# Five first gathers instead of two ahead of the last scatters, between the two runs of expert tiles

## The reference, cut to what matters

```python
x = x + _L0_conv_ref(_ln_c(x), ...)              # gate per channel
t = _to_tokens(x)                                # [2, 4096, 128]
t = t + _L0_ffn_ref(_ln_t(t), ...)               # experts, layer 0
x = _from_tokens(t, x)
x = x + _L1_conv_ref(_ln_c(x), ...)              # max-pools of 7 sizes, weighted per channel
t = _to_tokens(x)
t = t + _L1_ffn_ref(_ln_t(t), ...)               # experts, layer 1
# an expert: h = gelu(t @ W1[e] + b1[e]);  y = h @ W2[e] + b2[e], weighted, two of eight per token
```

## Time and profile before

| what | value |
|---|---|
| median of three executions | 989.05 us (987.12 to 992.66) |
| span of the profiled execution | 1121.3 us |
| TensorE matmul busy | 810.7 us, 72% of the span |
| GpSimd busy | 616.5 us, 55% |
| VectorE busy | 565.6 us, 50% |
| ScalarE busy | 516.3 us, 46% |
| mean granted TensorE clock | 0.844 of full speed |

### The profile page before, as it was taken

The page is one execution under the profiler, slowest core; times in us unless marked ns, Lnnn a source line. Parts: engine busy times, 40 slices in busy tenths (PEclk is TensorE's granted clock), DMA queues, the critical chain, the costliest instruction groups (busy, mean ns, idle before and its releaser), DMA issues.

```text
span 1121.3 us, 14549 instructions
## 1 busy us (share of the span) xinstructions
PE 810.7 (72%) x4233; PEld 683.7 (61%) x4233; DVE 565.6 (50%) x1308; ACT 516.3 (46%) x1407; POOL 616.5 (55%) x590
## 2 busy tenths in 40 slices
PE   1854389897867867986689488975996677796780
PEld 0434268785767655864678376854786565674670
DVE  8957902280500291999775296999681003300005
ACT  1405045562444445653266156643393443453563
POOL 1000266676655675788623755888646466665640
PEclk9876579997988888998589689998798788998895
DMA  8001344453565742553137733543256446555456
GB/s 317 1 0 57 123 149 125 139 156 98 174 193 187 248 156 87 172 158 118 38 109 236 254 110 109 183 138 102 65 162 220 135 128 201 194 157 174 133 162 225
DMA packets 54557, 165.23 MB, mean 147 GB/s; under 512 B 13632, under 2 KB 13645, under 8 KB 54224
## 3 DMA queue, kind: packets, MB, share of 16 engines
q1 hardware_dynamic: 36304, 128.87, 34.6%
q0 software_dynamic: 18176, 35.44, 10.8%
HBM read 134.89 MB, written 31.20 MB: 148 GB/s over the span
## 4 chain that ended last, share of the span: by engine, by line
PE 40%; DVE 26%; ACT 10%; another core or an unknown queue 10%; issue 8%; DMA 3%; POOL 2%; SPq 0%; POOLq 0%; ACTq 0%; DVEq 0%
PE h_ps L783 14%; PE yT_ps L796 12%; DVE state L1302 6%; DVE work L1288 4%; DVE work L1283 4%; ACT hT L596 4%; PE turn_ps L718 4%; PE acc_ps L735 3%; DVE tok L1252 2%; PE acc_ps L755 2%; DVE work L1296 2%; PE xT_ps L772 2%; ACT yT L607 1%; PE h_ps L886 1%
## 5 line engine op out<-in xcount | busy, mean ns | idle before, releaser
L511 POOL DMA_INDIRECT xg<-xn_rows,tile_rows x284 | 305.4, 1075 | 243.1 <-DVEq L1218 126.6
L520 POOL DMA_INDIRECT y_rows<-yr,tile_rows x284 | 306.9, 1080 | 236.1 <-ACT yr L616 147.5
L783 PE MATMUL h_ps<-xT,expert 128*128 128x256 f32 (+1 forms) x1376 | 317.7, 381 | 64.9 <-ACT hT L596 37.7
L796 PE MATMUL yT_ps<-hT,expert 128*128 128x256 f32 (+1 forms) x1376 | 300.2, 369 | 34.9 <-ACT yT L607 21.6
L596 ACT ACTIVATE hT<-h_ps,expert 128x256 f32<-128x256 f32 (+1 forms) x688 | 250.7, 451 | 154.7 <-PE h_ps L783 70.0
L783 PEld LDWEIGHTS h_ps<-xT,expert 128*128 128x128 f32 x1376 | 244.4, 213 | 103.1 <-issue 52.6
L796 PEld LDWEIGHTS yT_ps<-hT,expert 128*128 128x128 f32 x1376 | 247.5, 209 | 71.6 <-ACT yT L607 26.1
L1252 DVE SCALAR_TENSOR_TENSOR tok<-work,share,tok 128x128 f32<-128x128 f32 x224 | 61.2, 346 | 340.3 <-DMA work<-y_rows 336.9
L607 ACT ACTIVATE yT<-yT_ps,expert 128x256 f32<-128x256 f32 (+1 forms) x172 | 72.9, 444 | 170.3 <-PE yT_ps L796 92.4
L584 ACT ACTIVATE xT<-xT_ps 128x256 f32<-128x256 f32 x144 | 56.4, 392 | 117.8 <-PE xT_ps L772 59.7
L772 PE MATMUL xT_ps<-ident,xg 128*128 128x128 f32 x284 | 61.2, 298 | 58.2 <-DMA xg<-xn_rows,tile_rows 45.4
(11 more groups left out here) (210 smaller groups left out, 661.1 us busy)
## 6 DMA issues: line engine op xcount, KB each, us to landing
expert<-in_experts SPq DMA_DIRECT2D x172, 514.5 KB
work<-y_rows SPq DMA_DIRECT2D x24, 512.0 KB
xn_rows<-work SPq DMA_DIRECT2D x16, 512.0 KB, 4.4
xg<-xn_rows,tile_rows POOLq DMA_INDIRECT x284
y_rows<-yr,tile_rows POOLq DMA_INDIRECT x284
tok<-in_x_tokens SPq DMA_DIRECT2D x8, 512.0 KB, 6.9
state<-in_x SPq DMA_DIRECT2D x2, 2048.0 KB, 17.1
work<-y_rows SPq DMA_DIRECT2D x16, 256.0 KB, 6.1
```

Of the source, the lines that this page charges most:

```text
L511: pool.indirect_dma_start(xg[:, s, h, :], None, xn_rows[unit], bass.IndirectOffsetOnAxis(ap=tile_rows[unit % 2][:, at, 0, h:h + 1], axis=0)) \
L520: pool.indirect_dma_start(y_rows[unit], bass.IndirectOffsetOnAxis(ap=tile_rows[unit % 2][:, at, 1, h:h + 1], axis=0), yr[:, s, h, :], None ...
L783: mm = pe.matmul(h_ps[c // 2][:, c % 2, cols], expert[:, t.load(h) % W_RING, c * P:(c + 1) * P], xT[:, t.slot(2), cols], start=True, stop= ...
L796: mm = pe.matmul(yT_ps[:, cols], expert[:, t.load(h, d) % W_RING, HIDDEN + c * P:HIDDEN + (c + 1) * P], hT[:, s, c, cols], start=(c == 0), ...
```

## The change

`G_FIRST` goes. `begin` of a run's first unit gathers all five tiles at once, and nothing is left to gather at the top of the unit's loop. For unit 0 the order of the DMAs is what it was, as no scatter stands between. For unit 2 the gathers of tiles 2, 3 and 4 come ahead of the scatters of unit 1's tiles 33, 34 and 35. The number of DMAs and every other engine's program are the same.

```diff
-G_FIRST = 2
...
             for u in range(UNITS):
                 if begins_run(u):
                     if u == 0:
-                        begin(u, range(G_FIRST))
-                    for d in range(G_FIRST, G_AHEAD):
-                        gather(Tile(u, 0), d)
+                        begin(u, range(G_AHEAD))
...
                     if t.s == t.last + 1 and u + 1 < UNITS:
-                        begin(u + 1, range(G_FIRST))
+                        begin(u + 1, range(G_AHEAD))
                     if t.has(-S_BEHIND) and t.at(-S_BEHIND)[1] < TILES - 1:
                         scatter(t, -S_BEHIND)
                     if t.has(-2) and t.at(-2)[1] == TILES - 1:
                         scatter(t, -2)
```

## The result

The changed kernel takes 997.97 us (median of 18 executions, 993.95 to 1004.57), the kernel before, run beside it, 989.45 us (18 executions, 986.93 to 999.69). The ratio is 1.0082 with a 95% interval of 1.0057 to 1.0106: 8 us slower (5.6 to 10.5), where 7.3 were forecast. All 284 gathers and 284 scatters are still there; only their order at one place is new.

A forecast was written before the change was run, and what follows sets the result against it. No single engine bounds it: TensorE's and VectorE's paths meet at `gap`, VectorE's later. Its scatters' +7.57 us counts fully, TensorE's -5.24 us nothing; taken as 7.3, 989.05 + 7.3 = 996.4 us, range 986.5 to 999.5.

The forecast's parts named there:

- The clash in the queue: GpSimd's queue at the break before unit 2: gathers forward, TensorE -5.24 us; five scatters back, VectorE +7.57 us.
- Who sets `gap`: At unit 2's channel means: VectorE's path is already later by 3.5 us, so its full +7.57 us counts.
- VectorE's path: From unit 1's scatters through output loads, combine and normalising to the channel means: 674.3 before, 681.9 after, without stalls.
- The sum without stalls: Both paths to the channel means with profile stalls removed: TensorE 670.8, VectorE 674.3 before; 665.6 and 681.9 after.
- TensorE's path: From tile 2's gather through turning the normalised tokens at step 7 to the channel means: 670.8 before, 665.6 after.
- the lead of 3.5: At the channel means before the change: VectorE's path arrives 3.5 us after TensorE's path, without stalls.
- The choice of time base: Stalls at the break belong mostly to the profiled execution (1121.3 us against median 989.05); with them, 0 to -3.3 us.
- rival A: TensorE's path sets the channel means also when unprofiled: -0.3 to -3.3 us, about 987 us; chance 0.18.
- Step 25 and behind: TensorE waits 8.85 us for VectorE's state at step 25, so the shift passes on and nothing later takes it back.
- B: TensorE's idle at tile 2's gather is what counts: 5.24 us come off whole, 982 to 984 us; chance 0.04.
- C: VectorE's delay is hidden by slack behind the channel means, or gathers land late anyway: 989 us; chance 0.12.
- D: Output loads land later beside gathers of tiles 5 to 8, or TensorE cools down: +10 us, 999; chance 0.06.

The follow-up runs named there:

- three DMAs behind the scatters: Kernel before plus three spare scatters to unread DRAM, behind unit 1's last five scatters and ahead of tile 2's gather; ratio 1.0036.
- step 6 alone: Kernel before with only the turning of the normalised tokens moved from step 7 to step 6 of unit 2 (norm=6); ratio 0.9991.
- six and three DMAs behind the scatters: Kernel before plus spare scatters behind the five last scatters, ahead of tile 2's gather; six gave ratio 1.0056, three 1.0036.
- the six DMAs ahead: Kernel before plus six spare scatters to unread DRAM in front of unit 1's five last scatters, gathers of tiles 2 to 4 still behind; ratio 1.0048.
- three tiles first: Kernel before with three tiles instead of two gathered ahead of the scatters (G_FIRST = 3); ratio 1.0014.

## Why the prediction was right

**The clash in the queue.** As forecast, what was put forward for TensorE was put back for VectorE: 7.57 us in the sum, 18.43 - 10.94 = 7.49 at the loads and 7.56 at the combine. VectorE's wait was 25.41 us and not near 27, as it is 17.86 in the kernel before without stalls; it rose by 7.55. The early gathers ended tile 2's wait; tile 1's own rose from 1.01 to 1.81 us, which hadn't been costed.

**Who sets `gap`.** This step was the fragile one, and it held: VectorE's path, in 1.54 us of wait before `gap` in both kernels. Its size was wrong. The sum without stalls gave TensorE's path 54.5 us behind the last turn (670.8 - 616.26) and VectorE's 58.0 (674.3 - 616.26); measured were 53.0 and 54.05. The error lies mainly with VectorE's term, 4 us too long: its combine started at 16.29 instead of 17.76 us, the small steps between the statistics and the normalising took 4.13 and not 6.11 us (in the first profile they held gaps of up to 0.5 us that I hadn't taken out), and the way from the last normalised group to `gap` was 1.54 us and not the 2.03 of a pair. TensorE's step 1 ran faster than the 7.9 us I gave it (tile 2 turned at 568.45, tile 3 at 573.86), and tile 2 landed 1.4 us later. The forecast survived because a delay on the path that is already later counts fully, whether it leads by 3.5 or by 1.04 us. For a delay on TensorE's path the size of the lead matters: three DMAs behind the scatters moved `gap` by 2.47 us where the lead of 3.5 let 0.3 be expected.

**The choice of time base.** Reading the first profile as it stands gave 0 to -3.3 us, rival A's case. The stalls weren't part of the kernel: the second profile of before and that of the changed kernel have no "remote" wait. That choice carried the sign.

**Step 25 and behind.** TensorE waits there in all kernels, and the shift passes: 156.98 - 149.43 = 7.55 us. Behind it the changed kernel took 288.4 us to the span's end and the kernel before 289.8, so the profiled ends are 6.15 us apart, and the timed medians 8.5. Over the twelve profiles without stalls this stretch took 287.2 to 290.7 us, so the 1.4 us can't be told from its spread. That the timed loss came within 1 us of the forecast is partly luck: its interval reaches from 5.6 to 10.5 us, and the kernel before alone had medians up to 994.21 us in other sets. The 7.54 us at `gap` is what bears the forecast out.

**The rivals.** A fell with step 6 alone, which left `gap` where it was, and with the runs of six and three DMAs behind the scatters: TensorE does have something to spare, 1.04 us. (The middle of its price, -0.3 to -3.3 us, is 987.2 us; the range began at 986.5.) It was near in one respect: 1.04 us more on TensorE's side would have made its premise true. Not its price, though, for that the stalls had to be real, since the scatters' 7.57 us would still have outweighed so small a lead. B fell with the six DMAs ahead, where 14.5 us of TensorE's idle cost at most 0.7. The rule of the Trainium skill ("Perfetto Trace Analysis", Optimization Strategies) is, when TensorE is idle, to "optimize those engines that are blocking the critical path". The prediction took it without that condition, and so came to 983.8 us. Read whole, it doesn't ask for this change, and the runs agree with it: before `gap` the later path was VectorE's, by 1.04 us, and TensorE's wait for the gather lay on the other. C fell on step 25's wait and on tile 2's turn, which came without one. Of D no sign: the combine starts 5.42 us behind the loads, 5.35 in the kernel before, and TensorE's first eight products behind `gap` took 3.52 us at a granted clock of 0.53 (1.89 us further on, at 1.00), but inside the slack before step 25.

## What to carry to other kernels

When one queue feeds two engines, the order of its entries trades one path against the other: add up both paths to the point where they meet, and move an entry only from the later path's way. Ending a wait that is seen on one engine, even the busiest, can be worth nothing: it counts only as far as the other path, with the delay that the move puts on it, still arrives earlier. Where two paths are level within a microsecond, a gain of more than that comes only from cutting both, and a profile whose span is far above the timed median must be freed of its stalls, or taken again, before one reads which path leads.

## What the runs showed of the hardware that wasn't expected

**Stalls of a profile.** The first profile of before was 1121.3 us long against executions of 989 us, with 10% of its chain, some 112 us, in unknown waits; the second, of the same kernel, 989.9 us with none.

**The clock ahead of the break.** The last turn of unit 1 came anywhere from 545.75 to 555.43 us in the twelve profiles without stalls, though nothing ahead of it differs. The granted TensorE clock of the stretch before it goes with that. These are the stretches of the changed kernel and of the one with three tiles first: us, busy time of PE, PEld, DVE, ACT and POOL with instructions, granted clock, DMA share, GB/s.

```profile
480.00:545.00 65.00, 57.85 (x367) 54.41 (x368) 49.07 (x122) 40.05 (x116) 31.73 (x30) 0.76 0.42 131
```

```profile
480.00:545.00 65.00, 58.16 (x436) 54.71 (x436) 50.88 (x134) 44.77 (x134) 32.52 (x31) 0.91 0.51 160
```

In both TensorE had just waited for VectorE's mixed state of image 0, 8.91 us (until 481.97) and 8.89 us (until 478.87). With the low mean clock it got through 367 products, with the higher through 436, and unit 1 ended 9.6 us later, 3.1 of which it was behind already. Over the same 65 us of all twelve profiles, clocks of 0.76 (three) and 0.79 went with ends at 553.90 to 555.43 us, 0.82 to 0.84 (four) with 550.67 to 551.78, 0.88 (two) with 548.78 and 549.07, and 0.90 and 0.91 with 546.57 and 545.75: on the whole, the lower the mean clock, the later the end. This spread, about 1% of the time, is as large as the effect measured, so distances behind a common event told the experiments apart where the times couldn't. Why the mean clock differs from one execution to the next was not tried.
